# Differences of the first convolution's input kept in order of time, and matmuls that stream every fourth element

## The reference

```
x = x + conv(x, weight0, 9 taps, 4 groups of 32 channels) + c_weight0 @ cond + bias
x = x + agg_w1[b] @ x + agg_b1[b]
x = x + conv(x, weight2, 9 taps, 4 groups of 32 channels) + c_weight2 @ cond + bias
x = x + agg_w3[b] @ x + agg_b3[b]
```

## Time and profile before

| | |
|---|---|
| median of 3 runs | 2769.51 us (2768.08 to 2769.81) |
| profiled execution | 2769.83 us |
| its span, first to last instruction | 2768.0 us |
| TensorE, weight loads, VectorE, ScalarE busy | 98%, 47%, 78%, 37% |
| mean granted TensorE clock | 0.986 |

### The profile page before, as it was taken

How to read it: one execution, slowest core, us unless ns; L and a number is a source line. 1 busy time by engine, 2 the same in 40 slices (tenths; PEclk the granted TensorE clock), 3 DMA queues, 4 the chain that set the end, 5 groups by cost and what they waited for, 6 DMA issues and landing times.

```text
span 2768.0 us, 56616 instructions
## 1 busy us (share of the span) xinstructions
PE 2702.0 (98%) x24812; PEld 1304.8 (47%) x24812; DVE 2154.7 (78%) x815; ACT 1015.5 (37%) x596; POOL 36.9 (1%) x31
## 2 busy tenths in 40 slices
PE   6699999999999999999999999999999999999998
PEld 4244444444444444444444444444444444444454
DVE  4578788788788788787887887887887878878873
ACT  1233334334333334333343343333343333433433
POOL 5000000000000000000000000000000000000000
PEclk9699999999999999999999999999999999999999
DMA  4544444434434334334334334344344444443433
GB/s 151 199 148 129 129 121 136 127 116 142 123 114 147 119 114 151 114 114 152 114 114 152 114 117 148 114 126 139 122 127 130 129 128 122 134 128 117 142 94 107
DMA packets 185493, 357.06 MB, mean 129 GB/s; under 512 B 12714, under 2 KB 143794, under 8 KB 152634
## 3 DMA queue, kind: packets, MB, share of 16 engines
q1 hardware_dynamic: 184576, 352.37, 40.5%
q10 hardware_dynamic: 898, 4.39, 0.6%
HBM read 205.72 MB, written 150.99 MB: 129 GB/s over the span
## 4 chain that ended last, share of the span: by engine, by line
PE 96%; DMA 2%; DVE 1%; ACT 0%; issue 0%; ACTq 0%; SPq 0%; DVEq 0%
PE psum L312 64%; PE psum L320 32%; DMA mix_dram<-y 1%; DVE diff L511 0%; DVE y L560 0%; DMA select_sb<-select 0%; ACT y L439 0%; PE psum L273 0%; DVE y L569 0%; PE psum L302 0%; DMA mixw<-mix_dram 0%; ACT x L480 0%; ACT outb L467 0%; DVE att L531 0%; DVE y L542 0%
## 5 line engine op out<-in xcount | busy, mean ns | idle before, releaser
L312 PE MATMUL psum<-diff,prod_w 32*128 32x512 f32 x16384 | 1787.0, 588 | 10.4 <-DVE bias_table L550 5.5
L312 PEld LDWEIGHTS psum<-diff,prod_w 32*128 32x128 f32 x16384 | 847.9, 185 | 926.8 <-issue 876.0
L511 DVE TENSOR_TENSOR diff<-xin 128x2052 f32<-128x2052 f32 x256 | 985.4, 3892 | 0.0
L320 PE MATMUL psum<-y,mixw 32*128 32x512 f32 x8192 | 906.3, 589 | 18.2 <-DMA mixw<-mix_dram 13.7
L320 PEld LDWEIGHTS psum<-y,mixw 32*128 32x128 f32 x8192 | 427.9, 186 | 474.8 <-issue 468.7
L444 ACT COPY shared<-psum 128x2048 f32<-128x2048 f32 x256 | 478.1, 1868 | 380.8 <-PE psum L312 374.6
L566 DVE TENSOR_TENSOR y<-psum,shared 128x2048 f32<-128x2048 f32 x128 | 293.3, 2292 | 396.1 <-PE psum L312 396.1
L511 DVE TENSOR_TENSOR diff<-x 128x2055 f32<-128x2055 f32 x256 | 575.7, 2290 | 12.2 <-ACT x L480 12.2
L480 ACT ACTIVATE x<-psum,bias_now 128x2048 f32<-128x2048 f32 x128 | 252.7, 1974 | 644.4 <-PE psum L320 644.4
L467 ACT ACTIVATE outb<-psum,bias_now 128x2048 f32<-128x2048 f32 x128 | 252.0, 1969 | 633.4 <-PE psum L320 620.7
L569 DVE TENSOR_TENSOR y<-psum,shared 128x2048 f32<-128x2048 f32 x128 | 293.3, 2292 | 135.3 <-PE psum L312 135.3
(11 more groups left out here) (54 smaller groups left out, 81.5 us busy)
## 6 DMA issues: line engine op xcount, KB each, us to landing
xin<-x SPq DMA_DIRECT2D x128, 1024.0 KB, 6.6
out<-outb SPq DMA_DIRECT2D x128, 1024.0 KB, 4.8
mixw<-mix_dram SPq DMA_DIRECT2D x512, 128.0 KB, 5.2
mix_dram<-y SPq DMA_DIRECT2D x16, 1024.0 KB, 4.4
y<-experts ACTq DMA_DIRECT2D x2, 512.0 KB, 12.9
x<-conv_w ACTq DMA_DIRECT2D x1, 768.0 KB, 9.7
shared<-conv_w ACTq DMA_DIRECT2D x1, 768.0 KB, 11.2
diff<-expert_rows ACTq DMA_DIRECT2D x4, 144.0 KB
```

The source lines that it names most:

```text
L312: mm = pe.matmul(psum[:, half, g, :], prod_w[v][at, kind, s, :], diff[at, s, :, 0:R], start=first and s == 0, stop=last and s == PH - 1, s ...
L320: mm = pe.matmul(psum[:, half, r, :], mixw[m][at, b, g, :], y[m][at, :, g, b, :], start=g == 0, stop=g == GROUPS - 1)
L511: nc.vector.tensor_tensor(into(kind), in0, in1, op).then_inc(diff_ready[v], 1)
```

## The change

The differences of xin stay in the order of time: `diff_of_xin` reads runs of four phases (4 floats in a row, the next run 8 floats on) and writes them densely, as block, then phase. In diff0 the operand of the first convolution is then `p (b m s)`, and the matmuls of phase s read every fourth float. The second convolution's operands, the number of instructions, the weights and all waits stay as they are.

```
@@ product @@
-                diff = diff_of(v, kind).rearrange("p (s b m) -> p s b m", s=PH, b=PB)
+                diff = diff_of(v, kind).rearrange(("p (b m s) -> p s b m", "p (s b m) -> p s b m")[v], s=PH, b=PB)
@@ diff_of_xin @@
-                eighths = xin[:].rearrange("p (m c) -> p c m", c=BLOCK)
-                at = [eighths[:, PH * (q % 2):PH * (q % 2 + 1), q // 2:q // 2 + T - 1] for q in range(4)]
-                make_diffs(0, at, kinds, lambda kind: diff_of(0, kind).rearrange(
-                    "p (s c) -> p s c", s=PH)[:, :, 0:T - 1])
+                eighths = xin[:].rearrange("p (m c) -> p m c", c=BLOCK)
+                at = [eighths[:, q // 2:q // 2 + T - 1, PH * (q % 2):PH * (q % 2 + 1)] for q in range(4)]
+                make_diffs(0, at, kinds, lambda kind: diff_of(0, kind)[:, 0:PH * (T - 1)].rearrange(
+                    "p (m s) -> p m s", s=PH))
```

## The result

| | before | after |
|---|---|---|
| median | 2769.66 us (2768.08 to 2770.25, 4 runs) | 3725.18 us (3723.4 to 3726.46, 4 runs) |
| profiled execution | 2769.83 us | 3724.24 us |
| span | 2768.0 us | 3722.3 us |

The change costs 955.5 us by the medians (954.3 by the two profiled spans): ratio 1.3452, 95% interval 1.3435 to 1.3469.

The account below looks back on a forecast made before the run. TensorE's matmul chain was taken to bound the kernel, at 98% of the span; 2769.5 + 864 for stepped reads in the first convolution - 4.9 at the start gave 3629 us, range 2760 to 3830.

Parts of the forecast that it names:

- What bounds the loop: Steady loop: TensorE's convolution and mixing matmuls fill 2639 of 2768 us; the 410 us freed on VectorE are worth nothing there.
- VectorE's term: Four xin differences per step: each falls from 3892 ns to about 2290, freeing 410 us of VectorE.
- The start: Before the first front: three quicker differences let TensorE start at 36.4 to 36.8 instead of 41.39, gaining 4.9 us.
- GpSimd moves forward with VectorE: At the start: GpSimd's last prod_w, ending at 47.75 and slow because VectorE held GpSimd up, moves forward with VectorE.
- TensorE's term: First convolution's matmuls, reading every fourth float: a set of four takes 0.85 us for 0.43, +864 us over 2042 sets.
- I take the middle: TensorE's stepped stream: one element per 1.67 ns, the low-clock pace of the first sets; total 3629, chance 0.40.
- VectorE's row: Nearest SBUF evidence for TensorE's cost: stepped difference 3.79 us start to start, dense 2.20; ratio 1.72, or 1.85 ns per element.
- TensorE takes the step for nothing: Rival for the first convolution's stream: stepped reads cost TensorE nothing, only the start's gain remains; 2764.6 us, chance 0.34.
- VectorE's ratio: Rival for the first convolution's stream: a partial price, like VectorE's stepped-to-dense 1.72, +632 us; total 3397, chance 0.12.
- VectorE's time per element: Rival for the first convolution's stream: TensorE pays 1.85 ns per element as VectorE does, +1062 us; total 3826, chance 0.12.
- two hits: Skill's rule for SBUF reads: at least two hits on a 16-byte line are needed for full bandwidth; no price given.
- 4 fp32: Same skill note: calls this very step of the first convolution's stream free, leaving only the start's 4.9 us.

Follow-up runs that it names:

- VectorE's half alone: Changed kernel with xin differences in order of time, but matmuls streaming 512 neighbours as before the change; 2763.36 us, ratio 0.998 against the kernel before.

## Why the prediction was right, and where it was off

- **What bounds the loop.** Right. TensorE's chain fills it, and 403 us off VectorE gave nothing there: with VectorE's half alone all pieces kept their times.
- **VectorE's term.** Right: 2300 ns against 2290 forecast, from three of four elements being neighbours. The later price supports the reason: some 513 pieces of 1.75 ns are 0.9 us per input, well below the dense 2.3.
- **The start.** Right in place: forecast 36.4 to 36.8 for the first front, measured 36.46. Two small errors cancelled in it: the three differences took 8.79 us, more than the 8.46 that the prediction allowed at most, and they began at 27.22 and not 27.80. That GpSimd moves forward with VectorE, a half sentence in the prediction, turned out to be needed for all of the gain: the run with only the bias copies earlier gained nothing. The prediction's reason holds for the operations in front of it, not for the one named: the last prod_w takes 1.49 us before and 1.48 after; it is late and not slow.
- **TensorE's term.** The mechanism (a limit on how often a new place is reached) and the sign were right, the size was not: the step that failed is "I take the middle", one element per 1.67 ns. I had taken that from the pace of dense sets at the low clock, and it measured 1.75, 0.900 us a set for 0.853. The term is 961 us and not 864, hence 3725 for 3629; its own range, 3600 to 3660, missed too. Only the wide range, 2760 to 3830, holds the result, and 0.34 stood on no cost at all. The pace at the low clock was a property of TensorE and had nothing to do with the step, which runs at 0.90 at either clock; that the two lie within 5% of each other is luck. VectorE's row was the right neighbour: 1.85 ns per element start to start holds the fixed part of an instruction as well. Taking the difference of two sizes would have given the 1.73 to 1.77, which the trace before didn't have.
- **The rivals.** That TensorE takes the step for nothing (0.34) falls with the 28.80 us pieces. "VectorE's ratio" falls: a ratio of 1.72 is 1.75 ns over VectorE's dense pace, and TensorE's dense pace is shorter. "VectorE's time per element" was the right idea with a number 6% high; its 3826 is as far from the measured time as my 3629.
- **The rule cited.** The Trainium skill (SBUF — State Buffer, note on SBUF cachelines) has the unit right: pieces of 16 bytes, a penalty for each new one. Its "two hits" hold for VectorE (step 2 takes 2292 ns, no more than dense), and nearly for f32 on TensorE (0.450 against 0.429) and on ScalarE (2020 ns against 1898), not for bf16 on TensorE (0.451 against 0.216, which is the distance of the 31 records that the trace has of step 1). Its "4 fp32" as a free step is refuted by 0.899.

## What to carry to other kernels

Count the distinct 16-byte pieces that an access touches, borders included, and multiply by 1.75 ns; if that is more than the stream's dense time (0.84 ns per f32 and 0.42 per bf16 element on TensorE at 2.4 GHz), the pieces set the time. Where pieces hold unequal numbers of elements, this comes out too low on TensorE (0.45 us for the measured 0.533): there take for each piece the larger of 1.75 ns and the dense time of its elements, and add up. An engine with slack may pay for a change of layout, the one that bounds the loop may not: here VectorE's 410 us of stepped reads cost nothing in the loop, and stepped reads on TensorE cost 961. And when two chains meet at a start, look at who else a long instruction holds up before moving it.

## What the runs showed of the hardware that was not expected

- The price is one time for three engines: 1.74 to 1.77 ns per new 16 bytes on TensorE, 1.73 and 1.74 on VectorE, 1.72 on ScalarE, and on TensorE the same at 1.2 and 2.4 GHz. A second stepped input of the same instruction added nothing on VectorE (3773 ns against 3781), and VectorE's stepped reads beside TensorE's added nothing to its sets in the 3.1 us in which they met. Writes of VectorE pay about as much (3837 ns for 2052 scattered elements).
- The pieces don't average out on TensorE: uneven runs (three and one) take 0.533 us where even ones (two and two) take 0.450. A reader that waits for each piece by itself would take 0.55.
- Beyond four the step isn't quite indifferent: 0.899, 0.910, 0.919, 0.888 and 0.858 us for steps of 4, 5, 8, 12 and 16 floats. Why 16 is quicker stays open.
